# A ring of seven places for expert weights, their transfers and copies placed earlier, and one router step placed one head earlier

## The reference

```python
x = x + tanh(g_xattn[1]) * _L1_xattn_ref(_layernorm(x), ctx_512, ...)   # 16 heads, 4 batches
x = x + tanh(g_ffn[1]) * _L1_ffn_ref(_layernorm(x), Wr, Wg, Wu, Wd)

def _L1_ffn_ref(hidden_states, Wr, Wg, Wu, Wd):
    router_logits = jnp.einsum('bsh,he->bse', hidden_states, Wr)
    topk_logits, selected = jax.lax.top_k(router_logits, 2)
    router_probs = jax.nn.softmax(topk_logits, axis=-1)
    for e in range(8):
        w_e = jnp.where(selected == e, router_probs, 0.0).sum(-1, keepdims=True)
        g = jnp.clip(silu(hidden_states @ Wg[e]), -7, 7)
        h = (g * (hidden_states @ Wu[e])) @ Wd[e]
        out = out + h * w_e
    return out
```

## Time and profile before

| | us |
| --- | --- |
| median of 3 runs (lowest to highest) | 488.09 (485.65 to 489.6) |
| profiled execution, whole time | 487.2 |
| its span, first to last instruction | 485.4 |
| PE busy | 406.5 (84%) |
| DVE busy | 326.4 (67%) |
| ACT busy | 234.5 (48%) |
| POOL busy | 135.7 (28%) |

### The profile page before, as it was taken

The page is one execution under the profiler, slowest core; times in us unless marked ns, Lnnn a source line. Parts: engine busy times, 40 slices in busy tenths (PEclk is TensorE's granted clock), DMA queues, the critical chain, the costliest instruction groups (busy, mean ns, idle before and its releaser), DMA issues.

```text
span 485.4 us, 7933 instructions
## 1 busy us (share of the span) xinstructions
PE 406.5 (84%) x2691; PEld 334.2 (69%) x2691; DVE 326.4 (67%) x772; ACT 234.5 (48%) x515; POOL 135.7 (28%) x140
## 2 busy tenths in 40 slices
PE   1669896668799988998998898779898689999996
PEld 0334485336579777888777797669897468778885
DVE  0889259653799666999459995668662347555885
ACT  1022179233559647298455695552463165444322
POOL 5716000002601126302056011235177460000640
PEclk9999569796759999999999999998999799999999
DMA  6994700018001001001000010042242532211330
GB/s 159 292 341 144 99 1 1 0 52 273 22 2 45 1 1 44 2 23 23 2 22 24 1 45 1 2 109 76 78 132 105 177 113 85 88 65 46 92 106 22
DMA packets 30744, 35.37 MB, mean 73 GB/s; under 512 B 5713, under 2 KB 25793, under 8 KB 30449
## 3 DMA queue, kind: packets, MB, share of 16 engines
q1 hardware_dynamic: 26304, 28.11, 19.4%
q0 software_dynamic: 4400, 6.75, 6.3%
HBM read 25.61 MB, written 7.60 MB: 68 GB/s over the span
## 4 chain that ended last, share of the span: by engine, by line
PE 48%; DVE 26%; ACT 7%; issue 5%; DMA 2%; POOL 2%; SPq 0%; DVEq 0%; ACTq 0%; POOLq 0%
DVE egh L1727 11%; PE bank L1501 8%; PE bank L1363 6%; PE bank L1525 6%; DVE negm L1808 5%; PE bank L1178 4%; ACT Qs L972 3%; PE bank L1303 3%; PE bank L1322 2%; PE bank L1342 2%; PE bank L1343 2%; PE bank L1149 2%; PE bank L1127 2%; POOL xs L751 2%; PE bank L1164 1%
## 5 line engine op out<-in xcount | busy, mean ns | idle before, releaser
L1727 DVE RECIPROCAL egh<-egh 128x256 bf16<-128x256 bf16 x44 | 76.6, 1742 | 15.4 <-ACT egh L907 15.4
L1363 PE MATMUL bank<-kv,probs 128*128 128x128 f32 x512 | 67.5, 275 | 3.7 <-ACT negmT L964 2.9
L1363 PEld LDWEIGHTS bank<-kv,probs 128*128 128x128 f32 x512 | 62.5, 192 | 4.4 <-issue 3.5
L991 ACT ACTIVATE probs<-bank 128x512 f32<-128x512 f32 x64 | 36.9, 587 | 17.5 <-PE bank L1343 17.5
L1808 DVE TENSOR_REDUCE negm<-bank 128x2 f32<-128x512 f32 x64 | 41.4, 686 | 4.0 <-PE bank L1322 3.8
L1322 PE MATMUL bank<-Kh,Qs 128*128 128x256 f32 x128 | 32.7, 350 | 9.7 <-DVE negm L1808 4.8
L731 POOL TENSOR_SCALAR veps<-mv 128x2 f32<-128x2 f32 x12 | 2.7, 225 | 133.6 <-DVE mv L1559 133.6
L1342 PE MATMUL bank<-Qs,Kh 128*128 128x256 f32 x128 | 39.4, 329 | 0.0
L742 POOL TENSOR_TENSOR W<-w_in,W 128x512 fp32r<-128x512 f32 x24 | 30.0, 1282 | 32.9 <-issue 24.8
L1525 PEld LDWEIGHTS bank<-W,hTs 128*128 128x128 f32 x210 | 28.1, 189 | 15.5 <-DVE hTs L1962 9.9
L1525 PE MATMUL bank<-W,hTs 128*128 128x256 f32 (+1 forms) x210 | 32.9, 292 | 6.0 <-DVE hTs L1962 4.8
(11 more groups left out here) (205 smaller groups left out, 889.9 us busy)
## 6 DMA issues: line engine op xcount, KB each, us to landing
Qm<-Qs SPq DMA_DIRECT2D x32, 128.0 KB
xs<-f3A SPq DMA_DIRECT2D x1, 2432.0 KB, 9.7
Qm<-xs SPq DMA_DIRECT2D x19, 128.0 KB, 2.3
ys<-y SPq DMA_DIRECT2D x19, 128.0 KB, 2.0
w_q<-in_wq SPq DMA_DIRECT2D x2, 1024.0 KB, 17.9
w_o<-in_woT SPq DMA_DIRECT2D x1, 2048.0 KB, 10.9
w_in<-in_L_ffn_Wg SPq DMA_DIRECT2D x8, 256.0 KB, 4.2
w_in<-in_L_ffn_Wu SPq DMA_DIRECT2D x8, 256.0 KB, 2.7
```

Of the source, the lines that this page charges most:

```text
L991: done(act.activation(flat(pT[:, n % 3]), bank1(b, FILL_ST + h)[:], ACT.Exp), "p_ready")
L1363: ins = pe.matmul(bank_v(b, h // 2)[:, at:at + P], pT[:, n % 3, lt, t * P:(t + 1) * P], kv_all[:, frm:frm + P], start=(lt == 0), stop=(lt ...
L1727: done(dve.reciprocal(eg[:, j], eg[:, j]), "e1")
```

## The change

The ring `w_in` has seven places in place of four. SP issues loads 0 to 6 before the attention of batch 0, so the three loads that stood ahead of the last batch's first queries are gone from there. Loads 18 to 21 now stand ahead of the first `load_x`, and 22 and 23 behind its four fetches, with the fetches of tiles 4 and 5 behind them. In `run_all` the copies of expert 6 (`take(w)`) stand ahead of the first step of `t`, those of expert 7 right behind that step, and the last step of `heads[2]` stands one step of `a` earlier. POOL's program is as it was.

```diff
     take(heads[2])
     take(a, 3)
     take(heads[2])
+    take(a)
+    take(heads[2], None)
     take(a, 2)
-    take(heads[2], None)
-    take(a)
     take(p, None)
     for _ in range(3):
         take(w)
         take(a, 4)
     take(a, None)
-    take(t, 3)
     take(w)
     take(t)
     take(w)
-    take(t, 2)
+    take(t, 5)
     take(heads[3])
...
-        NWIN = 4
+        NWIN = 7
...
-            for k in range(NWIN, 7):
-                load_w1(k)
             for n in range(2):
                 queries_in(B - 1, n)
             for k in range(7, 10):
...
-            for k in range(13, 18):
+            for k in range(13, 22):
                 load_w1(k)
             for i in range(NXIN):
                 load_x(i)
-            for k in range(18, 3 * NE):
+            for k in range(22, 3 * NE):
                 load_w1(k)
-                if k == 21:
-                    for i in range(NXIN, 6):
-                        load_x(i)
+            for i in range(NXIN, 6):
+                load_x(i)
```

## The result

The changed kernel takes 485.02 us (median of 12 runs, 483.47 to 486.4), the kernel before 487.87 (12 runs on the same chip, 485.56 to 489.6). The ratio is 0.9953 with a 95% interval of 0.9931 to 0.9975: 2.3 us less. The forecast was 485.6.

What follows compares the result with a forecast made beforehand. PE was taken as the bound, except for waits on POOL and transfers ahead of the tiles and one hole between tiles. 2.17 (hole) + 0.30 (router) = 2.47 us won, giving 485.6; range 482.4 to 488.8.

Steps and rivals of the forecast that it cites:

- The hole: PE's gap between down products of tiles 1 and 2 shrinks from 5.02 to 2.85 us: 2.17 us won.
- Copies of expert 6 and 7: On ACT, expert 6's fit idle time ahead of the tiles, expert 7's ahead of tile 0's tanh: cost 0.
- The router: Router one head sooner: DVE's choice comes earlier; of 1.03 us of PE waits only 0.30 counts.
- the 0.30: PE's 0.30 us wait for DVE's choice at the plan's first product goes; counted as won.
- the 0.73: PE's 0.73 us wait at head 8 goes too, but does not count towards the time.
- The scatter held by the splits: POOL's scatter starts right behind expert 4's splits, so earlier slots buy nothing; the tiles hang on the scatter.
- Its start, 362.6 forecast: Sign to look for: scatter still starts at about 362.6 us, straight behind expert 4's splits.
- The sum: 2.17 + 0.30 = 2.47, say 2.5 us won over the whole kernel.
- The clock ahead of the tiles: Rival: PE's low-clock stretch shortens (2.7 us more won, 482.9; chance 0.09) or lengthens (2.7 lost, 488.3; 0.07).
- Tile 0 did not wait for matrix 23: Rival: ACT's late loads 22 and 23 delay tile 0; gain gone at 6.9 us landing; chance 0.08.
- the hole did not move: Rival: the 2.17 us return as other waits before tile 8, 487.8 to 488.1; chance 0.10.
- the scatter did not start by the full 1.03 us sooner: Rival: copies and attention pull everything 1.03 us earlier, 484.9; its chance is within the forecast's 0.66.

Runs made afterwards that it cites:

- the ring alone: Changed kernel with expert 6 and 7 copies and router step at their old places, keeping seven places and new transfer order: 483.91 us, ratio 0.9945 to the kernel before.
- the copies alone: Kernel before with only the copies of experts 6 and 7 in their new places, ring of four and old transfer order: 489.57 us, ratio 1.0062.
- the copies one tile later: Changed kernel with expert 7's copies behind tile 0's tanh in place of ahead of it: 485.27 us, ratio 0.9962 to the kernel before.
- the router undone: Changed kernel with batch 2's router step back in its old place: 485.57 us, ratio 0.9961 to the kernel before.
- the last two kernels of the series: Scatter and fetches early, DVE's last output addition behind the first tiles' remainders: 479.0 us; that kernel with expert 7's copies two tiles later on ACT: 477.61 us.
- scatter first: Changed kernel with POOL's scatter ahead of expert 4's splits, loads and copies moved to fit: 480.83 us, ratio 0.9867 to the kernel before.
- fetch first: Kernel with the scatter ahead of expert 4's splits, loads 19 and 20 also moved behind the first four fetches: 481.42 us, ratio 0.9881 to the kernel before.
- addition behind: Kernel with scatter and fetches early, DVE's last output addition and statistics moved behind the remainders of tiles 0 and 1: 479.0 us, ratio 0.9845 to the kernel before.
- expert 7's copies two tiles later: Kernel with scatter and fetches early and DVE's addition moved, expert 7's copies two tiles later on ACT: 477.61 us, ratio 0.9815 to the kernel before.
- router alone: Kernel before with only the router step moved: 487.21 us, ratio 0.9997.
- the ring of five: Changed kernel with five ring places in place of seven: 487.67 us, ratio 1.0014 to the kernel before.

## Why the prediction came out as it did

**The hole: right, and in its size.** 2.17 us forecast, 2.17 measured between tile 0 and tile 2. That the place in the ring was the cause, and neither ACT's time nor the tile's arithmetic, is shown by the ring alone (all of the gain, copies at their old place and without waits) and by the copies alone (slower). Whether the places or the order of transfers did more was not run apart; in the trace before, matrices 22 and 23 left when their places came free, at 391.12 and 392.38, long after the fetches ahead of them (383.23). The change is one only together: the earlier copies are harmless because of the seven places, not useful beside them. The prediction put the gain down to "both copies gone from tiles 1 to 3"; the ring alone shows that their going was not needed.

**Copies of expert 6 and 7: right, with less in hand than it seems.** The first were forecast from 371.1 and stand at 369.22: ACT's idle time itself began 1.8 us earlier. For the last two I had taken 384.1 and 385.6 as landing times, and ACT done at 386.2; with everything here 1.3 us earlier, that would be 384.9. ACT was done at 384.3, having waited 0.48 us. The splits of experts 5 to 7 follow in a row, from 376.48 and not 377.9. One reading was off by a split: matrix 20 needs the second of expert 4's splits, not only the first, and was issued at 360.02, still long before its use. The cost of 0 holds by the experiment with the copies one tile later. But in the profile with the router undone ACT waited 1.13 us for matrix 22, and the tanh came straight behind the copies (386.75), with none of the 0.52 us left over. And where the clock holds and PE is faster, the copies do cost: 1.2 us, by the last two kernels of the series. Their cover in the changed kernel was a product of 2.93 us at the half clock, which takes 1.65 at the full one.

**The router: the 0.30 somewhat low, the 0.73 the step that failed.** The wait at the plan was worth 0.45 and not 0.30, and 0.24 of it was lost again at the last scatter transfer. "It goes too" was wrong of the 0.73: 0.48 us is left. I had moved DVE's plan earlier by a head, and did not ask what POOL does in that time. Before, the plan took DVE 4.3 us, of which the last 1.9 ran behind expert 3's splits; now it takes 4.8, and only the last 1.4 run behind them. DVE's timeline, one instruction of the plan, before and then after:

```profile
356.13 0.21 DVE L1894 TENSOR_TENSOR rank<-rank,beyond 128x48 f32<-128x48 f32 x1
```

```profile
353.62 0.99 DVE L1890 TENSOR_TENSOR rank<-rank,beyond 128x48 f32<-128x48 f32 x1
```

POOL's splits of expert 3 after:

```profile
350.81 3.74 POOL L738 TENSOR_TENSOR W<-w_in,W 128x512 fp32r<-128x512 f32 x3 [10.19 <-issue]
```

Each takes 1.25 us, so they end at 352.06, 353.31 and 354.55; before, the last ended at 355.83. The long `rank` instruction ends at 354.61, 0.06 us behind the last split, and the plan's other long ones end within 0.11 us behind the end of a split too, before and after: DVE waits out the split that is running. The `wk` instructions, which had been under them, came free instead: 0.48 us in place of 1.45. The delay changed instructions. The Trainium skill, SBUF — State Buffer, section "SBUF: two separate sides", has a DVE instruction with two inputs from SBUF wait for a GpSimd instruction that reads SBUF, if that one started first, and the `rank` row is of that kind. The prediction named this rule for the tiles only, and not for the plan, where it bites. In the tiles it had the exception right: from tile 0's tanh on, DVE's instructions took 0.41 and 0.42 us beside POOL's splits, as before without them. The third pair's division comes at 356.10, 1.72 us earlier than before; 1.03 of that lies ahead of the router, so the router's step brought 0.69 where about 1 was forecast, while PE came to head 8 0.45 us earlier and not 0.30. It cost nothing, because POOL's scatter was held by its own splits, and PE's head 8 is not what the end hangs on there.

**The scatter held by the splits: right, and the most useful step.** It began 0.16 us behind them, both before and after, and not with the slots, which were ready 6 us sooner (355.23 and 361.40). Putting it ahead of the splits, with the loads and copies moved to fit, is worth 4.2 us, more than the change itself.

**Its start, 362.6 forecast, 361.40 measured:** 0.45 of the 1.46 us (rounded) is the router, and 1.03 lies ahead of it.

**The sum.** 2.47 was forecast. From the profile, without the 1.03 us from ahead of the router: 0.45 for the router, 0.24 given back at the scatter's last transfer, 0.30 of clock and fetch at the tiles, 2.17 for the hole: 2.7. Medians give 2.85, and the interval of the ratio 1.2 to 3.4. That the sum is so near is in part luck: the clock at the tiles, worth up to 2.7 us either way by the prediction, acted nearly as before.

**The rivals.** The clock ahead of the tiles fell as before (0.50 over 380 to 384), and was back slightly sooner: it was neither the 2.7 us won nor the 2.7 lost. It is not beyond reach: with DVE's addition moved, it stays whole, and the two last experiments profit. Tile 0 did not wait for matrix 23, the hole did not move in the changed kernel, and the scatter did not start by the full 1.03 us sooner through the router.

## What to carry to other kernels

When an idle time in the middle of a pipeline is named for a nearby engine, follow it back to the resource that came free late: here a place in a ring held back a transfer, three engines away from the wait, and the depth of the ring had to come before any reordering; the reordering alone was slower. Look in every in-order queue for work that nobody waits for, ahead of work that the end hangs on: splits ahead of a scatter, loads ahead of a fetch, an addition ahead of a tile, copies ahead of a tanh. Most became visible only when the one before was gone, and with the change they gave 9.0 us where the change alone gave 2.3. And if a step is moved, read what the other engines do at its new time: DVE's plan paid for POOL's splits there.

## What the runs showed of the hardware

**The granted clock falls or holds on small differences.** In four kernels PE went from attention to the tiles with waits of less than 2 us each. With 0.50, 0.59 and 0.26 us (scatter first) it fell to 0.50 over 380 to 382; with one of 1.78 (fetch first) it fell to 0.50 over 379 to 381; with 0.71 and a later 1.23 (addition behind) it stayed at 1.00 to 384, and with 0.71 alone (expert 7's copies two tiles later) to 388. The two levels are 1.2 and 2.4 GHz, and the low one made the first product of tile 0 2.93 us long, where it is 1.65 at the high one. The Trainium skill, TensorE: Matmul & The Clock Gate, section "Part 1: The HAM clock gate", calls the number of slow matmuls run-variable for one kernel. The mean clocks of this case's runs agree: 0.925 to 0.946 over nineteen runs of the kernel after. Its two profiles are alike (0.82 and 0.90 in the two stretches), and nothing here tells what picks a pattern.

**The last scatter transfer.** From its issue to that of the fetch, it was 2.44 to 2.45 us in the kernel before, the ring alone, the router undone and the copies alone, but 2.57 to 2.70 in four profiles with the router moved (after, twice; router alone; last copies later). With the router moved and the scatter and fetch first it was 2.43 to 2.45 again, so the router's place alone does not make it. No run told why.

**A fetch that follows a load.** The fetch of the first tile took 1.99 us in the chain of the kernel after, and 3.20 in the ring of five, where a load of 256 KB had been issued 0.5 us ahead of it. That distance alone does not make 3.20: with the scatter first a load stood 0.5 us ahead too, and tile 0 was turned 2.68 us after the issue.
